# Two graph layers: the touches of tiles 2 to 19 take their edges from a table in which every four rows begin with their own

## The reference, cut to what matters

```
dst = minimum((2500 * uniform(80000) ** 2.0).astype(int32), 19999)      # then sorted
h = relu(layernorm(x));  x = x + segment_sum((h @ W0)[src] * edge_weight[:, None], dst)
h = relu(layernorm(x))
x = x + segment_sum(norm[:, None] * (h @ W1.T + b)[col], row)           # row = dst and self loops
```

## Time and profile before

| | |
|---|---|
| three executions | 1643.34, 1647.43, 1656.27 us |
| the profiled execution | 1643.0 us, its span 1641.3 us |
| mean granted PE clock | 0.975 of full |
| busy: PE, DVE, POOL, ACT | 1507.0, 1064.6, 596.6, 443.1 us |
| touches: matmuls of L1379 | 1640 |
| sets of one-hots on DVE (L863) | 204 |
| stretch of the tile loop shown below | 510 to 1014 us |

### The profile page before, as it was taken

One profiled execution on the slowest core, in us unless ns is written; L12 is line 12 of the kernel. 1 busy time (PEld: TensorE's weight loads), 2 busy tenths in 40 slices (PEclk: granted clock), 3 DMA queues, 4 the chain that ended last, 5 costly groups with the idle time before them and its releaser, 6 DMA issues.

```text
span 1641.3 us, 28252 instructions
## 1 busy us (share of the span) xinstructions
PE 1507.0 (92%) x7964; PEld 804.4 (49%) x7965; DVE 1064.6 (65%) x1917; ACT 443.1 (27%) x855; POOL 596.6 (36%) x1530
## 2 busy tenths in 40 slices
PE   3978999967889999999999999989999999999997
PEld 2444555534444545445444554334645545546455
DVE  5887764448867778778687785389555456355442
ACT  5745544312122222222222221171202103002000
POOL 1135543435656778667677774000000000000000
PEclk9989999988989999999999999999999999999999
DMA  7202421174556666656665656571331412403102
GB/s 279 104 26 68 147 58 33 25 157 97 110 119 142 151 146 139 143 131 157 136 151 130 151 135 160 180 281 32 125 102 51 120 56 89 128 11 122 55 1 75
DMA packets 411488, 185.71 MB, mean 113 GB/s; under 512 B 376875, under 2 KB 393791, under 8 KB 411342
## 3 DMA queue, kind: packets, MB, share of 16 engines
q1 hardware_dynamic: 411342, 184.03, 42.7%
HBM read 76.45 MB, written 77.11 MB: 94 GB/s over the span
## 4 chain that ended last, share of the span: by engine, by line
PE 58%; DVE 12%; SPq 9%; DMA 7%; issue 6%; ACT 3%; DVEq 1%; POOL 1%; ACTq 1%; POOLq 0%
PE pair L1525 20%; PE pair L1580 13%; PE pair L1367 9%; PE pair L1433 9%; SPq L424 6%; PE pair L1379 5%; DMA a_scratch<-area 5%; DVE slots L868 2%; DVE slots L865 2%; DVE slots L869 1%; DVE area L920 1%; DVE slots L863 1%; SPq L415 1%; SPq L445 1%; DMA wstage<-c_scratch 1%
## 5 line engine op out<-in xcount | busy, mean ns | idle before, releaser
L1433 PE MATMUL pair<-h,area 128*128 128x512 f16 x2400 | 548.1, 382 | 4.3 <-issue 3.9
L1433 PEld LDWEIGHTS pair<-h,area 128*128 128x128 f16 x2400 | 232.8, 98 | 266.1 <-issue 17.2
L1525 PE MATMUL pair<-area,h 128*128 128x500 f16 x1600 | 341.9, 376 | 6.4 <-DVE h L1042 6.4
L1379 PE MATMUL pair<-slots 128*128 128x240 f16 x1640 | 205.9, 272 | 76.6 <-DVE slots L869 58.8
L611 POOL CAST fbuf<-etab 128x12 f16 (+2 forms) x644 | 205.8, 320 | 174.6 <-DVE slots L869 106.6
L1525 PEld LDWEIGHTS pair<-area,h 128*128 128x128 f16 x1600 | 156.1, 98 | 191.5 <-issue 11.7
L1379 PEld LDWEIGHTS pair<-slots 128*128 128x128 f16 x1640 | 158.4, 99 | 138.6 <-DVE slots L869 65.6
L1154 ACT ACTIVATE area<-pair 128x320 f32<-128x320 f32 x160 | 69.9, 437 | 542.7 <-PE pair L1379 317.7
L613 POOL TENSOR_TENSOR fbuf<-etab,negbase 128x4 f16 (+3 forms) x644 | 211.0, 328 | 0.5 <-issue 0.5
L1580 PE MATMUL pair<-wmat,area 128*125 128x512 f16 x960 | 209.0, 379 | 0.0
L863 DVE TENSOR_TENSOR slots<-iota_r,fbuf 128x640 f16<-128x640 f16 x204 | 106.0, 519 | 142.9 <-POOL fbuf L613 85.4
(11 more groups left out here) (195 smaller groups left out, 1117.5 us busy)
## 6 DMA issues: line engine op xcount, KB each, us to landing
c_scratch<-area SPq DMA_DIRECT2D x160, 160.0 KB, 2.3
a_scratch<-area SPq DMA_DIRECT2D x320, 80.0 KB, 2.3
xt<-x_scratch SPq DMA_DIRECT2D x20, 500.0 KB
out_x<-xt SPq DMA_DIRECT2D x20, 500.0 KB
xt<-in_x SPq DMA_DIRECT2D x19, 512.0 KB, 3.7
x_scratch<-xt SPq DMA_DIRECT2D x19, 512.0 KB, 3.3
wstage<-c_scratch SPq DMA_DIRECT2D x17, 500.0 KB, 4.5
slots<-c_scratch SPq DMA_DIRECT2D x17, 500.0 KB, 4.6
```

What stands on the lines that cost most here:

```text
L1379: return pe.matmul(dest, touches[:, t, 0:P], touches[:, t, P:CS], start=first, stop=last, skip_group_check=True)
L1433: last = pe.matmul(sum_pair(e)[:, half * H:(half + 1) * H], wts(e)[:, q, k, :], hpart(k, r)[:, half * H:(half + 1) * H], start=k == q == r ...
L1525: ins = pe.matmul(sums_of(c, f), hpart(k, q)[:, f * P:(f + 1) * P], counts, start=first and q == 0, stop=last and q == 1, skip_group_check ...
```

## The change

Quads 0 to 15 stay as they are. For windows 64 to 639 (tiles 2 to 19, `NA` = 576) the fields are selected once, during `support`, into a table `own_k`, `own_w` in SBUF with 8 touches for each later step. For a window whose first edges lie in chunk c, partition p takes chunk c's edge if that edge's row is the window's or a later one, and else the edge of chunk c+1; a second touch takes the chunk after. So a window's touches begin with its own edges. Windows 64 to 255 (quads 16 to 63) get two touches (`UA`), windows 256 to 639 one (`UB`); a step of eight touches then serves two quads.

The table is made so. In tile t = 5 of `support`, PE spreads the row of first chunks over all partitions and ACT copies it (576 columns); in t = 6, DVE makes seven one-hot matrices of it (`chunk_one_hots`). In t = 7, 8 and 10 to 15 (`OWN_AT`, four fields in two halves of 288 windows) PE picks the chunks' fields by products with them (`tables`, after k=5, in the PSUM pair of the transposes), ACT copies them out (`tables_out`, ahead of its w1 blocks and `window_out`) and DVE chooses per partition (`own_select`, after `support_share`). In t = 9 windows with edges left over are found and given to `further` with all their chunks (`select_windows`), in t = 16 the rest of `wtab` is computed (`later_windows`). `further` remains everywhere. POOL makes three casts of fields before `h_left(2)` for it, and ACT's `starts` waits for them. The first transposed load moves on SP from quad 8 to quad 13, behind waits for both tables. In the tile loops POOL copies a step's fields with two instructions; from quad 64 on, one-hots are built at even quads for two. PE's loop now starts at i = 0; it and DVE's are split at i = 3, where DVE waits for the touches of quad 63.

```diff
+    U0, UH, UP = (32, 16, 8, 8), 8, 4
     HQ = 4
...
+    UA, UB, QB = 2, 1, 64
     BT = 4
...
     assert N == NCK * CW == T * RW
+    VA, VB = 4 * PQ, 4 * QB
+    NA = NW - VA
+    NT = UA * (VB - VA) + UB * (NW - VB)
...
+        ROW_AT, HOTS_AT, SELECT_AT, TABLE_AT = 5, 6, 9, 16
+        OWN_AT = {7: (0, 0), 8: (0, 1), 10: (1, 0), 11: (1, 1), 12: (2, 0), 13: (2, 1), 14: (3, 0), 15: (3, 1)}
+        SCRATCH_AT = sorted([ROW_AT, SELECT_AT, *OWN_AT])
...
-                if w == QPT:
+                if w + STEP0 == TABLE_AT + 1:
+                    sp.wait_ge(own_ready, len(OWN_AT))
+                    sp.wait_ge(table_ready, 2)
                     load_weights(0, 0)
...
+            def own_step(k, s):
+                pool.wait_ge(hots_ready, k - 1)
+                at = bass.ds((k - PRE_STEPS) * 8, 8)
+                pool.tensor_copy(fbuf[:, s, 0:2], twice(own_k[:, :, at], [P, 2, 8, 2])).then_inc(own_fields, 1)
+                pool.tensor_copy(fbuf[:, s, 2:4], twice(own_w[:, :, at], [P, 2, 8, 2])).then_inc(own_fields, 1)
...
+            def own_hots(k, s, used):
+                dve.wait_ge(own_fields, 2 * (k - PRE_STEPS) + 2)
+                one_hots(k, s, used)
...
+                    if chunks == UA:
+                        own_hots(n + PRE_STEPS - PQ, q % 2, n - 1 + PRE_STEPS - PQ)
+                    elif q % 2 == 0:
+                        own_hots((td + PRE) * 4 + q // 2 + QB // 2 + PRE_STEPS - PQ, q // 2 % 2, steps_used(n - 2))
                     second_part(n - 1, 1 - q % 2, first and q == 0)
...
+            def chunk_one_hots():
+                dve.wait_ge(own_copied, 1)
+                for j in range(J + 2):
+                    ins = nc.vector.tensor_scalar(chunk_hot[:, j], chunk_row[0:EP], chunk_no[0:EP, j:j + 1], None,
+                                                  ALU.is_equal)
+                ins.then_inc(chunk_hots, 1)
...
+                lead = from_lead[:, 0:V_HALF[0]]
+                mask = from_first[:, at]
+                if f == 0:
...
+                    nc.vector.tensor_tensor(rest, rest, sums_row[:, at], ALU.add).then_inc(left_ready, 1)
+                if two:
+                    nc.vector.copy_predicated(singles, mask[:, two:V_HALF[0]], lead[:, two:V_HALF[0]])
+                    chain(nc.vector.copy_predicated(pairs[:, 1], mask[:, 0:two], pairs[:, 0]))
+                    last = nc.vector.copy_predicated(pairs[:, 0], mask[:, 0:two], lead[:, 0:two])
+                else:
+                    last = nc.vector.copy_predicated(singles, mask, lead)
+                last.then_inc(own_ready, 1)
...
+            def select_windows():
+                dve.wait_ge(own_copied, scratch_uses(SELECT_AT) + 1)
+                dve.wait_ge(own_ready, 2)
+                chain(nc.vector.tensor_scalar(forced, forced, 0.0, 50000.0, ALU.is_gt, ALU.mult))
...
+            def later_windows():
+                chain(nc.vector.tensor_copy(wcum[:, 0:NA], tab[:, 1, VA:NW]))
+                passes(VA, NW, wcum[:, 0:NA], wcum[:, 0:NA], wtmp, top[0:1, 10:11])
...
+                if w + STEP0 == HOTS_AT:
+                    chunk_one_hots()
+                if w + STEP0 in OWN_AT:
+                    own_select(w + STEP0)
+                if w + STEP0 == SELECT_AT:
+                    select_windows()
+                if w + STEP0 == TABLE_AT:
+                    later_windows()
...
-            with dve.Fori(1, T // 2 - 1) as i:
+            ONE_FROM = (QB // QPT - PRE) // 2
+            with dve.Fori(1, ONE_FROM) as i:
                 tile(i, 0)
                 tile(i, 1)
+            dve.wait_ge(step_used, steps_used(QB - 1))
+            with dve.Fori(ONE_FROM, T // 2 - 1) as i:
+                tile(i, 0, UB)
+                tile(i, 1, UB)
...
+            def tables_out(t):
+                act.wait_ge(own_sums, scratch_uses(t) + 1)
+                if t not in OWN_AT:
+                    dest = chunk_row if t == ROW_AT else forced
+                    act.activation(dest[:, 0:512], TP[:, 0:512], ACT.Copy)
+                    act.activation(dest[:, 512:NA], TP[:, 512:NA], ACT.Copy).then_inc(own_copied, 1)
+                    return
+                f, half = OWN_AT[t]
+                need(act, own_ready, own_at(t) - 1)
+                n, two = V_HALF[half], VB - VA if half == 0 else 0
+                act.activation(from_lead[:, 0:n], TP[:, 0:n], ACT.Copy)
+                if two:
+                    pairs = own[f][:, 0:UA * two].rearrange("p (v u) -> p u v", u=UA)
+                    act.activation(pairs[:, 1], TP[:, n:n + two], ACT.Copy)
+                    act.activation(pairs[:, 0], TP[:, H:H + two], ACT.Copy)
+                a = UA * (VB - VA) + (0 if half == 0 else V_HALF[0] - (VB - VA))
+                act.activation(own[f][:, a:a + n - two], TP[:, H + two:H + n], ACT.Copy).then_inc(own_copied, 1)
...
+            def own_step(k, s, u, pair, half=0):
+                pe.wait_ge(hots_ready, k + 1)
+                for t in range(4 * u):
+                    last = multiply(hot(s), half * 4 + t, win(pair, t // u), first=t // u % 2 == t % u == 0,
+                                    last=t % u == u - 1)
+                last.then_inc(step_used, 1)
...
+            def tables(t):
+                if t + 1 < T:
+                    pe.wait_ge(ht_ready, 2 * t + 4)
+                need(pe, own_copied, scratch_uses(t))
...
+                n = V_HALF[half]
+                at = half * V_HALF[0]
+                two = VB - VA if half == 0 else 0
+                for g, dest, width in ((0, TP[:, 0:n], n), (1, TP[:, H:H + n], n), (2, TP[:, n:n + two], two)):
+                    if not width:
+                        continue
+                    if f == 0:
+                        pe.matmul(dest, ones_h[0:1, :], neg_row[:, at:at + width], start=True, stop=False)
+                    for i, by_chunk in enumerate(own_parts[f]):
+                        for j in range(J):
+                            last = pe.matmul(dest, by_chunk[:, j * P:(j + 1) * P], chunk_hot[:, j - g + 2, at:at + width],
+                                             start=f > 0 and i == j == 0, stop=i == len(own_parts[f]) - 1 and j == J - 1)
+                last.then_inc(own_sums, 1)
...
+                    if chunks == UA:
+                        own_step(n + PRE_STEPS - PQ, g % 2, UA, pair)
                     else:
-                        step(n, steps_of(n)[0], g % 2, pair)
+                        own_step((2 * i + e + PRE) * 4 + g // 2 + QB // 2 + PRE_STEPS - PQ, g // 2 % 2, UB, pair, g % 2)
...
+                    if k == 5 and t in SCRATCH_AT:
+                        tables(t)
```

More of the change, by code:

```diff
@@ L881, in further @@
                     if isinstance(n, int) and n == 0:
[L882 removed]
+                        for w in range(2):
                             further_of(w, chunks_of(0, w))
+                        with dve.Fori(2, 4) as w:
+                            further_of(dve.snap(w, min_val=0, max_val=NW - 1), chunks_of(0, 2))
                     else:
                         with dve.Fori(0, 4) as w:
[L886 removed]
+                            further_of(dve.snap(n * 4 + w, min_val=0, max_val=NW - 1),
+                                       chunks_of(n) if isinstance(n, int) and n < PQ else 0)
             def further_of(v, u):
@@ L949, in moments_of_x1, with tile @@
                 ins.then_inc(stats_ready, 1)
-            def tile(i, e, first=False):
+            def tile(i, e, chunks=UA, first=False):
                 td = 2 * i + e
@@ L1262, in _ @@
                         std(MOMENTS_AT[w])
-                    window_out(w, w % 2, steps_before(w + 1), True)
+                    window_out(w, w % 2, steps_used(w + 1), True)
             sup_first(T - 1)
-            for td in range(UQ // QPT - PRE):
-                tile(td)
-            with act.Fori(UQ // QPT - PRE, T - PRE) as td:
+            act.wait_ge(table_ready, 2)
+            with act.Fori(0, T - PRE) as td:
                 tile(td)
@@ L1439, in dense, with tile @@
                     last.then_inc(agg_ready, 1)
-            def tile(i, e):
+            def tile(i, e, chunks):
                 for g in range(QPT):
```

265 lines of the change are left out of this document (178 added, 87 removed).

## The result

The changed kernel took 1669.8 us (median of four executions, 1667.3 to 1672.5) beside 1648.8 of the kernel before on the same chip: ratio 1.013, interval 1.011 to 1.016. I had forecast 1624 within 1606 to 1643. The time is outside the range, on the other side of the kernel before. The profiled execution took 1668.4 us. Its span is 1666.6, 25.3 more than the span before.

What follows compares the result with a forecast made beforehand. It took three latency-bound stretches per loop pass, where PE waits for one-hots, as the bound. Savings of 17.2 and 30.2 us against added costs summed to -22.5: 1643.0 to 1620.5, median 4.4 above; forecast 1624, range 1606 to 1643.

Steps and rivals of the forecast that it cites:

- The bound: Tile loop: three latency-bound stretches, where PE waits for one-hots, make a pass 69.9 us against 65.0 of PE work.
- The added cost of the table: `support`, up to quad 16: building the table, less shorter first-table passes, delays quad 16 by 23.4 us.
- The rival of selects that become the bound: Tiles 8 to 16 of `support`: DVE's selects hold up the one-hots, +58 us at 2.0 us each, 1682; chance 0.07.
- that of tables half as dear again: `support`: contention or a stretched w1 hand-over adds 8 to 22 us, 1632 to 1646; chance 0.24.
- DVE's jump still costs: Loop end, quad 0: rival that DVE's jump back stops costing with a shorter body, 1.7 us a pass, 1614; chance 0.08.
- Transfers don't hold the pass: Rows 1024 on: rival that DMA transfers hold the passes, which get no shorter, 1641; chance 0.06.
- Rows 1024 on: Tiles 8 to 19: four touches a quad save 2.87 us a pass, only outside the three stretches, -17.2 us.
- Costed at nothing: covered by the same stretches: Tile loops: halved one-hots on DVE and POOL's eight small copies a quad becoming two change nothing, 0 us.
- Tiles 2 and 3 and quads 32 to 39: Fewer touches, one set of one-hots a quad and no further touches of quad 33 save 30.2 us together.
- Tiles 4 to 7: Rows 512 to 1023 had 8 touches a quad and keep them, so 0 us.
- the crossing behind them: From loop to loop: DVE waits for quad 63's touches before building quad 64's one-hots, +1.5 us (0 to 3.8).
- The start's -1.8: Quads 16 to 20: four one-hot instructions fewer ahead of splitting quad 15, on which SP's store queue hangs, -1.8 us.

Runs made afterwards that it cites:

- e3_sp_after: Changed kernel with SP issuing each tile's two transposed loads behind the next tile's first and second store instead of ahead of both; 1597.1 us, ratio 0.970.
- e4_sp_before: Kernel before with SP's two transposed loads of a tile issued behind the next tile's first and second store; 1622.3 us, ratio 0.984.
- e10_unroll: Changed kernel with SP's transposed loads behind the next tile's first two stores, count adds on DVE and DVE's two tile loops written out; 1581.8 us.
- e7_dveadd: Changed kernel with the adds of counts to degrees moved from POOL to DVE for quads 15 to 159, nothing left out; 1645.9 us, ratio 0.999.
- e11_half_before: Kernel before with every second touch of quads 32 to 159 left out on PE, other engines' work as it was, no table; 1648.6 us, ratio 1.001.
- e1_fill: Changed kernel with twelve zero products added on PE in the wait before quad 4 of every tile from row 1024 on; 1654.1 us, ratio 1.005.
- e6_both: Changed kernel with POOL's count adds cut to one column in 80 and zero products filling the waits before quad 4; 1631.3 us, ratio 0.991.
- e2_twice: Changed kernel with each quad's four touches from row 1024 on issued twice, giving PE eight a quad again; 1675.6 us, ratio 1.018.
- e5_fewadds: Changed kernel with POOL's adds of counts to degrees cut to one column in 80 in the tile loops; 1651.4 us, ratio 1.002.

## Why the prediction was wrong, point by point

- **The bound: right.** Three stretches set by latencies. e3_sp_after and e4_sp_before show that SP's block was the cause of two of them, e10_unroll, beside e7_dveadd, that DVE's jump was that of the third.
- **The added cost of the table: right, its exactness in part luck.** Quad 16 starts 23.4 us later, as the sum of its terms has it. The terms one by one, from the starts of the tiles of `support`: ahead of tile 5 1.7 us earlier (forecast 1.2), tiles 5 and 6 +5.9 (5.0), 7 and 8 +11.3 (10.3), 9 +0.2 (0.8), 10 to 15 +9.2 (8.5). That is 24.9 late at the end of `support`, and 1.5 of it vanish in PE's wait ahead of quad 16 (6.6 us before, 5.1 now), which was in no term. The first split of w1 starts at 137.66 in tile 5 (forecast 139.1) and at 181.42 in tile 7 (forecast 176.6 and tile 5's 5.0 on top, 181.6). No wait of PE in tiles 10 to 15 is over 0.6 us. The rival of selects that become the bound, and that of tables half as dear again, are out.
- **The other rivals are out too.** DVE's jump still costs with the shorter body: the path from quad 6 to quad 0 is 8.5 us (8.8 before); without the one to quad 64, where no jump back stands, it is 8.8 (8.9). Transfers don't hold the pass: e10_unroll makes it in 61.6 us, with the DMA engines 79% busy. The change does what it says: the 1124 touches are 356 for quads 0 to 15 and exactly 768 for the rest, so none came from `further`. PE didn't set the pace either, at 73.3 us a pass.
- **Rows 1024 on: the step that failed.** "Fewer touches lengthen the waits inside them, and shorten the pass only outside them" took the stretches, and the dense blocks behind them, as fixed, and put no price on PE's clock. I forecast 67.0 a pass; before took 70.3 in the mean, so 67.4; measured 73.3. Of these 5.9 us, 1.7 are the three paths (49.4 us in sum instead of 47.7), drawn out by POOL's adds beside DVE, and 4.1 are quads 4: from their start to that of quad 5 are 6.3 and 5.7 us in the odd and the even tile, where 4.6 and 4.1 less 0.4 each were due. e11_half_before shows the second of these without any other edit, e1_fill and e6_both show it going when the wait is filled, and e2_twice shows the longer paths bringing it without a touch less, so the two losses don't simply add.
- **"Costed at nothing: covered by the same stretches"** was wrong for POOL's copies. They were not on the path, but they kept POOL's add off DVE's one-hots. e5_fewadds brings two paths back to 20.7 and 18.5.
- **Tiles 2 and 3 and quads 32 to 39: mis-sized. Tiles 4 to 7: wrong.** Forecast 190.5 us for quads 20 to 64, measured 201.9; without the adds 192.0. The largest part is quads 40 to 64. They had 8 touches, kept them and were put at 0, the crossing behind them at +1.5. They are 6.7 us longer: the waits at quads 44, 48 and 60 are 2.1 to 2.5 us instead of 0.7 to 1.8, and the three blocks behind them show 5.1, 5.1 and 4.8 us, 4.7 too much in sum. Without the adds these quads take 106.0 us, as before. The crossing costs nothing: PE doesn't wait at quad 64. The start's -1.8 was -0.5.
- **The range** reached only to rivals that left the loop's rule alone. (The sum itself gives 1620.5 + 4.4 = 1624.9, not 1624, which changes nothing.) The slower rival was put in the selects; that a saved 0.4 us could cost 2 was in no case, though the kernel before showed it, in the dense block behind the wait of 6.07 us of the earlier trace rows (timeline of PE):

```profile
457.75 5.44 PE L1433 MATMUL pair<-h,area 128*128 128x512 f16 x15 [1.29 <-issue]
```

## What to carry to other kernels

Work taken from an engine that waits on a fixed path makes the wait longer, and on PE a longer wait can be paid for once more in the clock of the block behind it: read the granted clock behind each wait before taking work away, and remove the path first. An engine that becomes idle does its next job earlier, so ask what it will then run beside. When a path starts with a queue's issue time, look for a place in that queue where nothing is due.

## What was not expected of the hardware

- How long PE had waited for a quad's first touch and whether the next 15 dense products were slow (over 3.5 us), over all fourteen profiles, quads 20 to 159, waits over 0.15 us: below 1.5 us 2 of 123, from 1.5 to 2 us 15 of 54, from 2 to 2.5 us 28 of 41, from 2.5 us on 52 of 58. Between, like waits end both ways, so the wait alone doesn't decide. The Trainium skill (TensorE: Matmul & The Clock Gate, the section on the gate) has the two levels, 1.2 GHz after idling and 2.4 GHz when busy, and says that the point of change varies from run to run; the rows agree on the levels, with a granted clock of 0.50 inside a block that shows 5.10 us where 3.40 is the rule.
- Two transposed loads of the same size took 16.2 us of SP's issue in one place, 18.5 and 30.6 in two others; beside what, was not tried.
- DVE's jump back took 3.8 us in the kernel before and 5.0 and 5.5 in two passes of e3_sp_after, where the DMA engines are busy 73% of the time instead of 63%. Whether that is the cause stays open.
